# A two-layer transformer-like block: the feed-forward's last product made by token, with the residual input and the attention norm's bias added to it by TensorE

## The reference, cut to what matters

```python
x = L0_attn_x
xn = _layernorm(x, axis=-1)
x = x + _L0_attn_ref(xn, ...) + _L0_ffn_ref(xn, ...)      # attn: _layernorm(static_out + o_dyn, o_norm_w, o_norm_b)
xn = _layernorm(x, axis=-1)                               # ffn:  ... ; return _tlin(h, w3_w, w3_s)
x = x + _L1_attn_ref(xn, ...) + _L1_ffn_ref(xn, ...)
```

## Time and profile before

| | us |
|---|---|
| runs of the kernel | 943.64, 941.96, 939.7 (median 941.96) |
| profiled execution, its own time | 942.68 |
| profiled execution, its span | 941.0 |

### The profile page before, as it was taken

How to read it: one execution, slowest core, us unless ns; L and a number is a source line. 1 busy time by engine, 2 the same in 40 slices (tenths; PEclk the granted TensorE clock), 3 DMA queues, 4 the chain that set the end, 5 groups by cost and what they waited for, 6 DMA issues and landing times. The chain is left out here.

```text
span 941.0 us, 12422 instructions
## 1 busy us (share of the span) xinstructions
PE 767.8 (82%) x2956; PEld 494.0 (52%) x2956; DVE 779.7 (83%) x1573; ACT 556.0 (59%) x1049; POOL 627.2 (67%) x572
## 2 busy tenths in 40 slices
PE   5388888189999999989999998105899999999996
PEld 3244333057666766656666766002555655555654
DVE  5588888199999999999999999943888888888885
ACT  3477887268888888867787875003443443443431
POOL 0077888467878787867878772004878878778873
PEclk9999999669999999999999999656999999999999
DMA  5145555820503205050310501032013213213101
GB/s 144 44 169 198 203 201 190 190 46 12 113 22 72 62 17 117 23 111 13 77 56 11 123 0 45 11 109 93 0 57 99 68 56 105 62 56 109 59 16 30
DMA packets 121656, 75.02 MB, mean 80 GB/s; under 512 B 73490, under 2 KB 99996, under 8 KB 121628
## 3 DMA queue, kind: packets, MB, share of 16 engines
q1 hardware_dynamic: 119420, 72.98, 27.5%
q10 hardware_dynamic: 2208, 1.74, 0.6%
HBM read 41.14 MB, written 33.55 MB: 79 GB/s over the span
## 5 line engine op out<-in xcount | busy, mean ns | idle before, releaser
L1358 POOL TENSOR_TENSOR l_kv<-l_qkv 128x1024 f32<-128x1024 f32 x64 | 125.0, 1953 | 22.7 <-PE l_ps_s L1568 22.7
L944 POOL TENSOR_TENSOR f_hl<-f_h,f_hh 128x512 fp32r<-128x512 f32 x64 | 81.9, 1297 | 73.8 <-ACT f_hh L1064 73.8
L1136 PE MATMUL f_ps<-f_hh,w_hi 128*128 128x512 f32 x256 | 108.3, 423 | 0.4 <-ACT f_b L1053 0.4
L1136 PE MATMUL f_ps<-f_gh,w_hi 128*128 128x512 f32 x256 | 103.5, 404 | 4.6 <-POOL f_gl L944 4.5
L919 DVE TENSOR_TENSOR r_pg<-r_rec,r_pt 128x512 f32<-128x512 f32 x128 | 88.5, 692 | 19.6 <-ACT r_kb L1029 13.1
L925 DVE TENSOR_REDUCE r_rec<-r_pg 128x64 f32<-128x576 f32 x128 | 97.4, 761 | 7.2
L1411 ACT ACTIVATE l_qkv<-l_ps_q 128x512 f32<-128x512 f32 x64 | 38.2, 597 | 103.8 <-PE l_ps_q L1555 103.7
L1489 DVE TENSOR_TENSOR l_qs<-l_ps_s,l_qd 128x1024 f32<-128x1024 f32 x64 | 78.1, 1221 | 25.8 <-PE l_ps_s L1568 24.7
L952 POOL TENSOR_TENSOR f_g<-f_a,f_b 128x512 f32<-128x512 f32 x64 | 82.1, 1295 | 20.2 <-ACT f_b L1053 20.2
L928 DVE TENSOR_TENSOR r_kw<-r_rec,r_kb 128x512 f32<-128x512 f32 x128 | 88.5, 691 | 4.4
L933 DVE TENSOR_REDUCE r_gain<-r_kw 128x128 f32<-128x512 f32 x128 | 87.8, 686 | 4.4
(11 more groups left out here) (184 smaller groups left out, 1979.6 us busy)
## 6 DMA issues: line engine op xcount, KB each, us to landing
p_x<-in_L_attn_x_dram SPq DMA_DIRECT2D x16, 256.0 KB, 3.0
scratch_xnT<-p_xnT SPq DMA_DIRECT2D x16, 256.0 KB, 3.1
scratch_K<-p_kout SPq DMA_DIRECT2D x16, 256.0 KB, 2.9
scratch_fac<-p_fac SPq DMA_DIRECT2D x16, 256.0 KB, 2.0
scratch_R<-p_rr SPq DMA_DIRECT2D x16, 256.0 KB, 2.0
scratch_P<-p_pp SPq DMA_DIRECT2D x16, 256.0 KB, 2.1
f_x<-scratch_xnT SPq DMA_DIRECT2D x16, 256.0 KB, 2.8
r_p<-scratch_P SPq DMA_DIRECT2D x16, 256.0 KB, 4.8
```

The source lines that it names most:

```text
L944: pool.tensor_tensor(lower, full, upper.bitcast(F32), ALU.subtract).then_inc(done, 1)
L1136: nc.tensor.matmul(bank, c.w_hi[:, weights[k], :], upper[k], start=k == 0, stop=False)
L1358: pool.tensor_tensor(dst, k, v, ALU.mult).then_inc(kv_ok, 1)
```

## The change

The feed-forward's last product is turned round. Before, `w3` was the stationary operand and the 512 tokens the moving one, so the result lay by channel; ACT took it from PSUM with the scale `w3_s` and the bias `o_norm_b`. Now 128 tokens of `f_e` are the stationary operand and `w3` (scaled by `w3_s` in `setup`, on DVE) the moving one, so the result lies by token. Into the same PSUM bank PE first multiplies rows of ones by `ob_rows` (the bias in an upper and a lower part, over 512 columns), and adds the input `x_t`, which SP loads by token, as a product with the identity. ACT copies the sum out. The DRAM tensor `scratch_ffnT` becomes `scratch_xf`, which holds input plus feed-forward plus bias. The second layer loads three tensors for a sequence and not four; PE's four transposes and DVE's addition of `branches` are gone, and POOL's `residual` reads the loaded tensor. The load of a sequence now waits for `x1_ok` where it waited for `xf_ok`.

```diff
+                dve.wait_ge(tr_done, NG)
+                dve.wait_ge(loaded, NL)
+                dve.tensor_tensor(c.w3[:, :, :], ps[(NG - 1) % 2][:, :, :], s3[:, :].unsqueeze(1).to_broadcast([P, NB, P]),
+                                  ALU.mult).then_inc(w3_done, 1)
...
+                link(dve.tensor_copy(o_hi[:, :], o_bias[0:2 * ROW, :]))
+
+                def over_tiles(rows):
+                    return rows.unsqueeze(1).to_broadcast([rows.shape[0], NT, P])
+
+                dve.tensor_copy(c.ob_rows[0:ROW, :, :], over_tiles(o_hi[0:ROW, :].bitcast(F32)))
+                dve.tensor_tensor(c.ob_rows[ROW:2 * ROW, :, :], over_tiles(o_bias[ROW:2 * ROW, :]),
+                                  over_tiles(o_hi[ROW:2 * ROW, :].bitcast(F32)), ALU.subtract)
+                dve.tensor_copy(c.ob_rows[2 * ROW:P, :, :], over_tiles(o_bias[2 * ROW:P, :]))
...
+                def load_xt(q):
+                    sp.dma_start(x_t[:, :, :], io["L0_attn_x"][q.row(), :, :].rearrange("b (t p) d -> p (b t) d", p=P)).then_inc(xt_in, 16)
+
+                def store_y(q, more=True):
                     sp.wait_ge(y_ok, q.count(1, 3))
-                    sp.dma_start(scr["ffnT"][q.row(), :, :].rearrange("b p t -> p (b t)"), y_t[:, :]).then_inc(y_out, 16)
+                    if more:
+                        load_xt(q.back(-1))
+                    sp.dma_start(scr["xf"][q.row(), :, :].rearrange("b (t p) d -> p (b t) d", p=P), y_t[:, :, :]).then_inc(y_out, 16)
 
                 load_x(Slot(0))
+                load_xt(Slot(0))
                 load(0, 0)
...
                 def result(q):
                     act.wait_ge(y_mm, q.count(1, 1))
                     act.wait_ge(y_out, q.count(16, 16))
-                    act.activation(y_t[:, :], y_at[:, :], ACT.Identity, scale=c.s3[:, :], bias=c.ob[:, :]).then_inc(y_ok, 1)
+                    act.activation(y_t[:, :, :].rearrange("p t d -> p (t d)"), y_at[:, :], ACT.Copy).then_inc(y_ok, 1)
...
                 def output(q):
                     pe.wait_ge(e_ok, q.count(NB, 3 * NB))
-                    for k in range(NB):
-                        ins = nc.tensor.matmul(y_at[:, :], c.w3[:, k, :], e_f[:, k, :], start=k == 0, stop=k == NB - 1)
+                    pe.wait_ge(xt_in, q.count(16, 16))
+                    nc.tensor.matmul(y_at[:, :], c.one_rows[:, :], c.ob_rows[:, :, :].rearrange("p t d -> p (t d)"), start=True, stop=False)
+                    for t in range(NT):
+                        tokens = slice(t * P, t * P + P)
+                        nc.tensor.matmul(y_at[:, tokens], c.ident[:, :], x_t[:, t, :], start=False, stop=False)
+                        for k in range(NB):
+                            ins = nc.tensor.matmul(y_at[:, tokens], e_f[:, k, tokens], c.w3[:, k, :], start=False,
+                                                   stop=t == NT - 1 and k == NB - 1)
                     ins.then_inc(y_mm, 1)
...
                 def load(l):
                     if l.turn is not None or l.off >= 2:
-                        sp.wait_ge(xf_ok, l.count(1, -1))
-                    by_token = io["L0_attn_x"][l.row(), :, :].rearrange("b (t p) d -> p (b t) d", p=P)
+                        sp.wait_ge(x1_ok, l.count(1, 0))
                     sp.dma_start(w_in[l.slot][:, :], scr["W"][l.row(), :, :].rearrange("b p t -> p (b t)")).then_inc(in_ok[l.slot], 16)
                     sp.dma_start(fac_in[l.slot][:, :], scr["fac"][l.row(), :, :].rearrange("b p t -> p (b t)")).then_inc(in_ok[l.slot], 16)
-                    sp.dma_start(f_in[l.slot][:, :], scr["ffnT"][l.row(), :, :].rearrange("b p t -> p (b t)")).then_inc(in_ok[l.slot], 16)
-                    sp.dma_start(x_in[l.slot][:, :, :], by_token).then_inc(in_ok[l.slot], 16)
+                    sp.dma_start(xf_in[l.slot][:, :, :], scr["xf"][l.row(), :, :].rearrange("b (t p) d -> p (b t) d", p=P)).then_inc(in_ok[l.slot], 16)
...
                 def residual(l):
-                    pool.wait_ge(xf_ok, l.count(1, 1))
+                    pool.wait_ge(in_ok[l.slot], l.loads())
                     pool.wait_ge(xn_ok, l.count(1, 1))
                     pool.wait_ge(yw_ok, l.count(1, 2))
-                    pool.tensor_tensor(x1[l.slot][:, :, :], yw[:, :, :], xf[:, :, :], ALU.add).then_inc(x1_ok, 1)
+                    pool.tensor_tensor(x1[l.slot][:, :, :], yw[:, :, :], xf_in[l.slot][:, :, :], ALU.add).then_inc(x1_ok, 1)
...
-                def branches(l):
-
-                    dve.wait_ge(in_ok[l.slot], l.loads())
-                    dve.wait_ge(f_tr, l.count(1, 1))
-                    dve.wait_ge(x1_ok, l.count(1, 1))
-                    dve.tensor_tensor(xf[:, :, :], x_in[l.slot][:, :, :], ps_x[:, :, :], ALU.add).then_inc(xf_ok, 1)
...
-                def branches(l):
-                    pe.wait_ge(in_ok[l.slot], l.loads())
-                    pe.wait_ge(xT_ok, l.count(1, 1))
-                    for t in range(NT):
-                        ins = nc.tensor.transpose(ps_x[:, t, :], f_in[l.slot][:, t * P:(t + 1) * P], c.ident[:, :])
-                    ins.then_inc(f_tr, 1)
-
                 def normed(m):
                     pe.wait_ge(xn_ok, m.count(1, 3))
-                    pe.wait_ge(xf_ok, m.count(1, 1))
+                    pe.wait_ge(xT_ok, m.count(1, 1))
```

More of the change, by code:

```diff
@@ L81, in constants @@
     c.ow = sb("ow", [P, P])
-    c.ob = sb("ob", [P, 1])
+    c.ob_rows = sb("ob_rows", [P, NT, P], F32R)
     c.eps_ln = sb("eps_ln", [P, 1])
@@ L162, in setup @@
             add(dst[:, :], io[name].rearrange("(o p) -> p o", p=P))
-        add(c.s3[:, :], io["L0_ffn_w3_s"].rearrange("(p o) -> p o", o=1))
+        add(s3[:, :], io["L0_ffn_w3_s"].partition_broadcast(P))
         add(c.ow[:, :], io["L0_attn_o_norm_w"].partition_broadcast(P))
-        add(c.ob[:, :], io["L0_attn_o_norm_b"].rearrange("(p o) -> p o", o=1))
+        for row in (0, ROW):
+            add(o_bias[row:row + 1, :], io["L0_attn_o_norm_b"].unsqueeze(0))
         for n, name in enumerate(("L0_attn_lam_logit", "L0_attn_eta_raw", "L1_attn_gamma")):
@@ L1513, in step @@
                     at(l, scale1)
-                    at(l, branches)
                     at(n, scores, 2)
```

32 lines of the change are left out of this document (17 added, 15 removed).

## The result

The changed kernel takes 950.94 us (median of 4 runs, 949.46 to 951.88) against 941.46 us for the kernel before on the same chip (4 runs, 939.70 to 943.64). The ratio is 1.0098, 95% interval 1.0073 to 1.0124: slower, by 9.5 us or 1%. The profiled execution took 949.46 us, the shortest of its four, and its span is 947.8 us; that of before took 942.68 us, 1.2 above its median, and its span is 941.0. So the pair of profiles shows 6.8 us and not 9.5; where the other 2.7 us lie, no trace shows. The 6.8 us split up at three instructions that both traces have: ACT's first `lay_r`, DVE's last instruction of the recurrence's block, and PE's transposes of `l_y_t` for the last sequence.

The account below looks back on a forecast made before the run. The prediction saw PE and ACT's feed-forward loop running at DVE's pace, and POOL's loop as the second layer's floor. Setup +2.5, start +1.2, block +8.0 and second layer -5.8 made +5.9 us: 948 us, range 940 to 952.

Parts of the forecast that it names:

- likeliest case: Whole kernel: the prediction's own sum of its terms, 945 to 951.5 us, given chance 0.50.
- the bound of 946.7: Whole kernel: a median above this counts as slower, about 0.5% (4.7 us) being what a measurement can tell; chance 0.58.
- Setup, +2.5: Setup: DVE's added w3 multiplication, bias part and ob_rows instructions lengthen the queue ending the stage by 2.5 us (1.8 to 3).
- Start, +1.2: Start of the recurrence's block: the first x_t load stands ahead of six awaited loads, +1.2 us (0.4 to 1.5).
- The last product, +1.23 a turn: Feed-forward output on PE's loop: from 3.45 to 4.68 us, adding 1.23 us a turn.
- +8.0 at DVE: Save of phase 24: lag 14.8 us, less 2.98 (gap), 1.46 (half clock) and 2.30 (spare), makes DVE 8.0 us late.
- Rival (a): Recurrence's block: it hides the longer turn, lag under 2.3 us at phase 24's save; 940 us, chance 0.17.
- The forecast's other term, POOL's copy: Recurrence's block, segment 5: 9 x 1.23 - 4.44 = 6.6 us late, earlier than the save and contained in its 8.0.
- Second layer, -5.8: Second layer: twelve steps 0.32 us shorter each, 3.9 us, plus 1.9 us from the first steps; -5.8 us, down to -11.
- The step of 17.18: Second layer: POOL's loop stays at 17.18 us, so a step falls from 17.50 to that.
- Rival (b): Second layer: the step follows PE down to 16.74 us, 5.3 us less in all; 942.7 us, chance 0.13.
- rival (d): Last product: weight loads in the open add 4.4 us a turn, 53 us over twelve; about 1001 us, chance 0.03.

Follow-up runs that it names:

- pool_sum_setup: Changed kernel with x added by POOL instead of PE, DVE's added setup work given to POOL, w3's copy on ACT: 938.00 us, 0.9961 of the kernel before.
- xt_once: Changed kernel with x_t loaded once, behind the first two segments' loads, instead of 16 times: 949.27 us, 1.0068 of the kernel before.
- pe_six: Kernel before with six extra short products on PE ahead of output's own, nothing else changed: 952.46 us, ratio 1.0102.
- pe_three: Kernel before with three extra short products on PE ahead of output's own: 944.30 us, ratio 1.0024.
- pool_sum: Changed kernel with x added to y_t by POOL instead of by PE's four identity products: 941.85 us, 0.9997 of the kernel before.
- spare_each_step: Changed kernel with four transposes of a constant tile put back on PE in every second-layer step: 950.38 us, 1.0093 of the kernel before.
- second_only: Kernel before with only the changed second layer and by-token scratch tensor, x and bias missing from the sum: 937.00 us, ratio 0.9950.
- first_steps: pool_sum_setup with four constant-tile transposes on PE in each of the second layer's first three steps: 937.54 us, 0.9952 of the kernel before.
- no_sum: Changed kernel whose output leaves out the ones product and four identity products, so no x or bias: 941.99 us, 0.9996 of the kernel before.
- warm: pool_sum_setup with unread PE products, 120 behind the last output and 28 at the second layer's start: 940.81 us, 0.9979 of the kernel before.

## Why the prediction was right

**The forecast: +5.9 us, 948 us.** The measured medians differ by 9.5 us; 950.94 us lies in the likeliest case's own range of 945 to 951.5 and above the bound of 946.7. The profiled pair, on which the sum was built, moved by 6.8 us. That the sum comes so near is in part luck: the start was put 2.4 us too high, the block 1.7 and the last stretch 1.4 us too low.

**Setup, +2.5.** Right: DVE's last row moved by 2.34 us, and pool_sum_setup takes it back.

**Start, +1.2.** Right in kind: xt_once and the changed kernel differ by 1.1 us from the first issue to `lay_r`, before and changed by 0.7. The two terms together should have moved `lay_r` by 3.7 us, and the profiled pair shows 1.3. Where `lay_r` stands differs between profiles of the same setup: 183.6 to 185.6 in the kernels with DVE's old or moved setup, 186.1 to 188.0 in the others. The means of the two groups are 2.0 us apart, the rest is scatter of the stage between. In the profiled pair that stage took back most of the setup's 2.34 us: the first issue behind it moved by 0.62 us only (174.27 to 174.89).

**The last product, +1.23 a turn.** The mechanism was right, the size too small. The output was put at 4.68 us and took 4.71. The four products before were put at 3.45 us, from passes in the chain of the second layer. In the turn the distance from PE's first product of `output` to its next stage's first is 3.13 us before (434.50 to 437.63), which looks like a growth of 1.6. But the row of that next product cannot be read so: the one behind it stands 0.63 us later before (438.26) and 0.32 us later in the changed kernel (447.42). Read to this second one, `output` grew from 3.76 to 5.03 us, by 1.27, close to the forecast's 1.23. Another 0.08 us lies in front of it (it starts 1.16 us behind the turn's first product before, 1.24 after), and 0.04 behind. pe_six added 1.39 and arrived with 1.39.

**+8.0 at DVE.** Right, with the turn's real size: 12 x 1.39 = 16.7, less 2.98 and 1.46, gives 12.2 at the save of phase 24, measured 11.9; less 2.30, 9.9, measured 9.7. That half the clock behind the long gap goes away with the gap was right for the changed kernel. The forecast's other term, POOL's copy, is as good: 9 x 1.39 - 4.44 = 8.1 us, and DVE is 7.9 us later behind it. The forecast had called it contained in the save's 8.0, which holds at this size. At a small one it does not: in pe_three the copy alone carries the loss, 9 x 0.69 - 4.44 = 1.8 us, measured 1.9. Rival (a), that the recurrence hides it, falls for this turn and holds for one of 24.45: pool_sum's block is no longer than that of before.

**Second layer, -5.8.** The sum was right by luck, since both of its parts were wrong. The twelve steps gave 5.7 us where 3.9 were forecast, the first steps 0 where 1.9 were; of the 0.7 us for the shorter load, 0.2 arrived at the first transposes and none at sequence 3. The step of 17.18 was read as a floor from the one step in which PE did not wait for `l_y_t`. It was not POOL's shortest: from `l_yw` to `l_y_t` POOL took 8.08 us there and 7.93 in the changed kernel. In both, `l_qd` starts 7.10 us behind `l_yw`; in the step of the forecast POOL then started `l_y_t` 0.15 us later than in the changed kernel, with no wait listed, and in the other eleven steps it waited 0.28 to 0.92 us for the load. So the forecast had the right wait, the load's, and the right loop, but took the best step for the loop's own length. That those 0.15 us are the load too is likely and not shown. Rival (b), that the step follows PE down to 16.74, falls: spare_each_step puts PE's 0.44 back and the step stays. PE's idle time in front of `l_y_t`, forecast at about 0.4 us, shows only as 0.20 us on the weight load; in spare_each_step the 0.44 us of work found room in several places of the step.

**The weight loads, rival (d).** Twenty f32 products of 128 columns and one of 512 took 4.71 us, so one with its weights takes 0.22 us. By the rule quoted from the Trainium skill, "TensorE: Matmul & The Clock Gate", section "Packing small matmuls — row/col tiling", they would have taken about twice that by the forecast's estimate; the trace does not agree.

**Not in the forecast.** The last stretch of the second layer is 1.4 us longer. PE's final eight passes took 2.08 us at 941.67, at half clock from 941.4 on; they took 1.17 us in the kernel before. No experiment was aimed at it. Over the thirteen profiles, where these passes took 1.2 to 1.5 us the stretch is 50.9 to 51.8 us long, and where they took 1.7 to 2.1 it is 51.5 to 52.8, also with the same second layer (51.0 in second_only, 52.7 in pool_sum). So the half clock explains part of it, and the rest stays open.

## What to carry to other kernels

When two loops run at the same pace, time added to the one is free only up to the slack of the nearest handover. For each handover, multiply the addition by the turns before it and take off what the loop has in hand there. Here there were two: POOL's copy after nine turns, with 4.44 us in hand and nothing to spare, so 0.49 us a turn are free (an estimate from these numbers); and the save after twelve, with 4.44 and 2.30, so 0.56. Additions of 0.44, 0.69 and 1.39 us bear it out. The engine with a gap in each turn (here GpSimd, 4.7 us) could take the work at no cost that the trace shows, where the engine with the fast instruction for it could not. An engine's row without a wait is no proof that it is the bound: split the step into its pieces in both kernels and see which one changed, or put back a known amount of work and see whether the step moves.

## What the runs showed of the hardware

Work taken off PE changed when its clock rose. With four transposes in each of the first steps the full clock came 27 to 31 us behind the end of the recurrence (before, pe_six, pe_three, first_steps, spare_each_step), without them 38 to 40 us (changed, second_only, no_sum, xt_once, pool_sum, pool_sum_setup). The earlier rise was not worth what it looks like: in before, first_steps and spare_each_step the clock fell again for 3.4 to 7 us at about 38 us, and sequence 3 stands at 56.9, 57.0 and 57.9 us, against 56.9 in the changed kernel. Filling an idle PE with products did not pay in warm: the clock fell about 5 us after the filling stopped (617.6 to 622.8), and the products that followed ran at half of it for their first 5.5 us and held up the real ones.

The time at which the stage behind `prepare` begins scatters by 2 us between profiles of kernels with the same code up to there, at different stretches of half clock. That is as much as the setup's whole term, so it had to be read in its own rows rather than at the next stage's start.
